# A router's threshold search in 16 turned rows per expert, two bits per level, with places from running sums

## The chip, the core and the metric

The kernel runs on one core of a Trainium2 chip. The metric is the device time of one execution in microseconds (us). The engines are PE (TensorE, matmul), DVE (VectorE), ACT (ScalarE), POOL (GpSimd) and SP (SyncE, which only issues DMAs).

## What is computed

Two layers, each a cross-attention and a feed-forward part with residuals, on `x` of 8 x 512 x 256. The last part is the one that the change touches: a mixture of 8 experts over all N = 4096 tokens, each expert taking at most 512 of them.

```python
probs = softmax(xf @ gate_w.T)                      # [4096, 8]
# per token: experts by falling probability, until their sum reaches 0.9
select_prefix = arange(E)[None, :] <= k_idx[:, None]
R_sorted = where(select_prefix, p_sorted - rank, -1e9)
# per expert: the 512 tokens of highest R (ties: the earlier token)
topC = argsort(-R, axis=0)[:C, :]
scores_sel = where(assign_mask & keep, probs, 0)
h = gelu(einsum('nd,efd->enf', xf, w1)); y_e = einsum('enf,edf->end', h, w2)
y = einsum('ne,end->nd', scores_sel, y_e)
```

## The kernel before

The program is a row of blocks: `setup` (constants), `mlstm_gates`, `mix_and_mlp`, `attention` (the longest), `logits`, `router`, `experts`. Between two blocks all engines meet. Inside a block each engine has its own written order, and semaphores order them against each other. On DVE the helper `v(ins)` lets every instruction wait for the one before.

Tokens lie as 128 partitions x NT = 32 tiles; `key` holds for each token and expert the value rank + 1 - p (low is good), and a huge value (FAR) where the token does not choose the expert. The router (L1237 to L1448) works thus:

- Softmax (L1351 to L1356), then pairwise comparisons of the 8 probabilities of a token into `pair_a` (L1363, L1365, and a memset of the diagonal, L1367); its sum is the rank, and its product with the probabilities, summed, is the probability mass `before` this expert (L1370 to L1372). L1374 to L1380 make `key`.
- PE turns `key` (L1317), so that an expert is 32 rows of 128 keys, four experts in each of two halves: `key_rows` [128, 2, 128].
- A search of 27 levels, one bit each, finds for each expert the largest threshold below which fewer than 512 keys lie. A level is on DVE two counts (L1393, a compare that also sums along its row), on PE one matmul with the 0/1 matrix `group` that adds the rows of an expert (L1323), on DVE the decision (L1399) and the next candidate (L1401). Beside levels 8 to 23 PE turns one half of an expert's weights each (`turn_weights`, L1312, four transposes), which ACT copies out (L1299).
- The thresholds are spread to all partitions (L1407 to L1411). Then, in the unturned layout, the keys below the threshold are counted (L1384, L1385), and `ranks` (L1418 to L1423: two matmuls, eight running sums) runs twice: once to pick the ties that still fit, once for each chosen token's place. L1438 to L1446 split the place into `chunk` (place / 128) and `slot`.

`experts` (L1451) copies `slot` to bf16 (L1648), builds on DVE one-hot matrices per expert (L1595 to L1610), gets the token list by matmul, gathers the token rows by indirect DMA on POOL (L1490), runs the two maps on PE, and adds the rows to the output by indirect DMA on POOL (L1501).

## Time and profile before

| what | value |
|---|---|
| median of 3 runs | 1900.68 us (1900.4 to 1904.55) |
| the profiled execution | 1900.8 us, of which its span is 1899.1 us |
| PE busy / DVE / ACT / POOL | 1708.0 / 1205.3 / 844.2 / 619.8 us |
| mean granted TensorE clock | 0.93 of full speed |

The busy shares are means over all blocks; the change lies in one of them. The rows of a timeline give the start of an instruction in us from the span's start, its length, engine, line, operation and tiles; in brackets stands how long the engine had been idle before it, and who ended that.

### The profile page before, as it was taken

The numbers are of one execution on the slowest core, as the hardware profiler recorded it, in microseconds if no ns is written. First come the engines' busy times: TensorE is split into PE (matmuls) and PEld (weight loads), VectorE is DVE, ScalarE is ACT, GpSimd is POOL, SyncE is SP. The second block draws the span as 40 slices with busy tenths as digits, with TensorE's granted clock in tenths as the row PEclk, the third lists the DMA queues.
The fourth block names the chain that finished last, engine by engine and source line by source line (L and its number), as shares of the span: only waits on it lengthen the run. The fifth ranks groups of instructions, "written<-read, shape, count | busy, mean of one in ns | idle before, by whom it ended". The sixth has DMA issues, their size and how long they took to land. (4 is left out here: it accounts for less than half of the span.)

```text
span 1899.1 us, 26206 instructions
## 1 busy us (share of the span) xinstructions
PE 1708.0 (90%) x8900; PEld 1157.0 (61%) x8900; DVE 1205.3 (63%) x2743; ACT 844.2 (44%) x1870; POOL 619.8 (33%) x745
## 2 busy tenths in 40 slices
PE   6569999996999999999999999999999999674484
PEld 4456677764666666666666666666666666472252
DVE  5443444431677777777777777777777777657761
ACT  3223443331555555555555555555555555211110
POOL 2143544440233333332323323333233233200385
PEclk9659999998999999999999999999999999855697
DMA  7100000003223222232231322323222223070154
GB/s 252 20 12 23 12 12 1 1 1 102 59 53 67 47 66 64 48 67 52 61 67 45 67 56 56 67 45 67 60 52 67 49 63 67 23 236 14 38 86 57
DMA packets 66658, 109.47 MB, mean 58 GB/s; under 512 B 16088, under 2 KB 48096, under 8 KB 66528
## 3 DMA queue, kind: packets, MB, share of 16 engines
...
q8 instruction: 72, 1.18, 0.3%
q14 instruction: 58, 0.48, 0.1%
...
## 5 line engine op out<-in xcount | busy, mean ns | idle before, releaser
L1018 POOL TENSOR_SCALAR at_Pr<-at_Pr,at_rinv 128x512 f32<-128x512 f32 x512 | 355.8, 695 | 824.4 <-DVE at_rinv L1045 824.4
L997 ACT ACTIVATE at_Pr<-at_ps,at_nmax 128x512 f32<-128x512 f32 x512 | 351.9, 687 | 522.6 <-DVE at_nmax L1040 521.0
L1040 DVE TENSOR_REDUCE at_nmax<-at_ps 128x1 f32<-128x512 f32 x512 | 351.1, 686 | 138.1 <-PE at_ps L905 127.3
L905 PE MATMUL at_ps<-at_k,at_q 128*128 128x512 f32 x1024 | 420.6, 492 | 9.6 <-DMA at_k<-at_k_own 7.9
L916 PE MATMUL at_ps<-k_ident,at_Pr 128*128 128x128 f32 x2048 | 310.7, 274 | 4.4 <-POOL at_Pr L1018 4.4
L916 PEld LDWEIGHTS at_ps<-k_ident,at_Pr 128*128 128x128 f32 x2048 | 249.3, 140 | 94.2 <-POOL at_Pr L1018 33.2
L1052 DVE COPY at_PT<-at_ps 128x512 f32<-128x512 f32 x384 | 261.5, 681 | 0.0
L905 PEld LDWEIGHTS at_ps<-at_k,at_q 128*128 128x128 f32 x1024 | 174.3, 190 | 128.9 <-issue 119.4
L926 PE MATMUL at_ps<-at_PT,at_V 128*64 128x512 f32 x1024 | 235.4, 602 | 0.9 <-DVE at_PT L1052 0.9
L1045 DVE RECIPROCAL at_rinv<-at_rsum 128x1 f32<-128x1 f32 x512 | 83.4, 163 | 175.0 <-ACT at_Pr L997 173.0
L926 PEld LDWEIGHTS at_ps<-at_PT,at_V 128*64 128x64 f32 x1024 | 68.2, 137 | 122.5 <-issue 121.4
L936 PE MATMUL at_ps<-at_wo,at_oT 128*128 128x256 f32 x512 | 131.6, 380 | 0.8 <-ACT at_oT L983 0.8
L446 PE MATMUL mm_ps<-mx_w,mm_hT 128*128 128x256 f32 x512 | 120.9, 382 | 0.0
L436 PE MATMUL mm_ps<-m_xnT,mx_w 128*128 128x512 f32 x256 | 112.8, 599 | 1.3 <-ACT m_xnT L589 1.3
L893 PE MATMUL at_ps<-at_w_rest,m_ctxT 128*128 128x128 f32 x896 | 109.2, 275 | 0.0
L884 PE MATMUL at_ps<-m_xnT,at_w_rest 128*128 128x512 f32 x224 | 106.3, 597 | 0.0
L884 PE MATMUL at_ps<-m_ctxT,at_w_rest 128*128 128x512 f32 x224 | 105.4, 593 | 0.0
L893 PEld LDWEIGHTS at_ps<-at_w_rest,m_ctxT 128*128 128x128 f32 x896 | 104.5, 192 | 0.0
L446 PEld LDWEIGHTS mm_ps<-mx_w,mm_hT 128*128 128x128 f32 x512 | 93.7, 190 | 16.6 <-issue 5.3
L1027 DVE SCALAR_TENSOR_TENSOR at_q<-at_ps,m_b_all,at_q 64x512 fp32r<-64x512 f32 x128 | 96.0, 750 | 8.6 <-ACT at_q L966 5.7
L997 ACT ACTIVATION_READ_ACCUMULATOR at_Pr<-at_ps,at_nmax 128x1 f32 x512 | 98.5, 192 | 0.0
L936 PEld LDWEIGHTS at_ps<-at_wo,at_oT 128*128 128x128 f32 x512 | 87.4, 190 | 8.3 <-ACT at_oT L983 1.7
...
## 6 DMA issues: line engine op xcount, KB each, us to landing
at_k<-at_k_own SPq DMA_DIRECT2D x256, 256.0 KB, 4.3
...
```

Source lines behind the costliest of these rows:

```text
L436: ins = pe.matmul(ps[:, H_BANK + f % 4, :], w1_s[:, k, P * f:P * f + P], xnT_all[:, k, b * S:b * S + S], start=k == 0, stop=k == DC - 1)
L446: ins = pe.matmul(ps[:, Y_BANK + t // 2, D * (t % 2):D * (t % 2) + D], hT[:, f, P * t:P * t + P], w2_s[:, f, :], start=f == 0, stop=f == F ...
L884: ins = pe.matmul(ps[:, A_BANK + k, :], weights(k, d, hp), src[:, d, b * S:b * S + S], start=d == 0, stop=d == DC - 1)
L893: ins = pe.matmul(ps[:, A_BANK, P * t:P * t + P], ctxT_all[:, d, b * S + P * t:b * S + P * t + P], weights(2, d, hp), start=d == 0, stop=d ...
L905: ins = pe.matmul(ps[:, S_BANK + j % 2, :], q2[:, u % 2, h, q:q + P], k2[:, u % 2, h, part, :], start=part == 0, stop=part == 1)
L916: ins = pe.transpose(ps[:, T_BANK + j % 2, P * t:P * t + P], Pr[:, j % 4, P * t:P * t + P], c["ident"][:, :])
L926: ins = pe.matmul(ps[AD * h:AD * h + AD, O_BANK, :], V[:, u % 2, t, AD * h:AD * h + AD], PT[:, u % 2, h, t, :], start=t == 0, stop=t == TP ...
L936: ins = pe.matmul(ps[:, Y_BANK - half, D * (t % 2):D * (t % 2) + D], oT[:, P * t:P * t + P], wo_s[:, u % HP, :], start=True, stop=True)
L997: act.activation(Pr[:, j % 4, :], ps[:, S_BANK + j % 2, :], ACT.Exp, bias=nmax[:, j % 4:j % 4 + 1], accum_out=rsum[:, j % 4:j % 4 + 1]).th ...
L1018: pool.tensor_scalar(Pr[:, n % 4, :], Pr[:, n % 4, :], rinv[:, n % 4:n % 4 + 1], 1.0, ALU.mult, ALU.mult).then_inc(s["pn"], 1)
L1040: dve.tensor_reduce(nmax[:, j % 4:j % 4 + 1], ps[:, S_BANK + j % 2, :], AX.X, ALU.max, negate=True).then_inc(s["nmax"], 1)
L1052: dve.tensor_copy(PT[:, u % 2, j // TPB, :, q:q + P], ps[:, T_BANK + j % 2, :].rearrange("p (t q) -> p t q", t=TPB)).then_inc(s["pt_v"], 1)
```

## The change

It touches `setup`, `router` and the first lines of `experts`; the kernel's other lines and all DMAs stay.

- `setup`: the constants `lower`, `ones_bf` and `earlier` go; `group` (now 0/1 blocks of 16 rows) and a new `group_ahead` (the rows in front, within a block) are made on POOL by three dependent selects and cast on DVE.
- The diagonal of the pair matrix (now `ahead`) is cleared by one memset while ACT computes the exponentials. Of the product with the probabilities POOL takes 14 of the 32 tiles and DVE 18; `key` takes three instructions besides these sums, one of them ahead of `before`, where it took six behind it.
- `key` is turned by parity of the tile: all 8 experts lie in 128 rows, 16 rows of 256 keys each.
- The search first decides one bit (4.0), then 13 levels of two bits: three candidates at once, three counts over 256 keys, one matmul of three columns, a compare that sums the three answers into a digit, and one addition to `T`. From its seventh matmul on PE turns both halves of an expert's weights per level.
- The thresholds need no spreading. In the turned rows two counts (below, equal) give masks, two running sums over 256 give places within a row, two small matmuls give each row's offset, and two pairs of matmuls with the identity turn the places back and add the two parts. Three instructions make `chunk` and a bf16 `slot_b`, and the first instruction of `experts` on DVE adds 1 to the comparison line.

```diff
 def setup(nc, c):
...
-                dve.memset(c["group"][:, :], 0.0).then_inc(s["cleared"], 1)
-                dve.wait_ge(s["cleared"], 1)
...
+                dve.wait_ge(s["made"], GROUP)
+                dve.tensor_copy(c["group"][:, :], same[:, :])
+                dve.wait_ge(s["made"], AHEAD_OF)
+                dve.tensor_copy(c["group_ahead"][:, :], ahead[:, :])
...
+                blocks = same[:, :].rearrange("p (g r) -> p g r", r=NT // 2)
+                pool.affine_select(out=blocks, in_=blocks, compare_op=ALU.is_ge, fill=0.0, base=0,
+                                   pattern=[[-NT // 2, E], [0, NT // 2]], channel_multiplier=1
+                                   ).then_inc(s["made"], 1)
+                pool.wait_ge(s["made"], HALF)
+                pool.affine_select(out=blocks, in_=blocks, compare_op=ALU.is_ge, fill=0.0, base=NT // 2 - 1,
+                                   pattern=[[NT // 2, E], [0, NT // 2]], channel_multiplier=-1
+                                   ).then_inc(s["made"], 1)
+                pool.wait_ge(s["made"], GROUP)
+                pool.affine_select(out=ahead[:, :], in_=same[:, :], compare_op=ALU.is_gt, fill=0.0,
+                                   base=0, pattern=[[1, P]], channel_multiplier=-1).then_inc(s["made"], 1)
...
-        STEPS = list(range(2, -25, -1))
+        FIRST = 2
+        LEVELS = list(range(FIRST - 2, -25, -2))
...
+            @block.gpsimd
+            def _(pool):
+                pool.wait_ge(s["ahead"], 1)
+                pool.tensor_tensor(weighed[:, 0:BY_POOL, :, :], ahead[:, 0:BY_POOL, :, :],
+                                   prob[:, 0:BY_POOL, :].rearrange("p t (a e) -> p t a e", a=1).broadcast_to(
+                                       [P, BY_POOL, E, E]), ALU.mult).then_inc(s["weighed"], 1)
...
                 pe.wait_ge(s["key"], 1)
-                for half in range(2):
-                    ins = pe.transpose(ps[:, 2, P * half:P * half + P],
-                                       key_e[:, HALF * half:HALF * half + HALF, :].rearrange("p e t -> p (e t)"),
-                                       c["ident"][:, :])
+                by_parity = key_e[:, :, :].rearrange("p e t -> p (e t)").rearrange("p (m r) -> p r m", r=2)
+                for r in range(2):
+                    ins = pe.transpose(ps[:, KEY_BANK, P * r:P * r + P], by_parity[:, r, :], c["ident"][:, :])
                 ins.then_inc(s["key_ps"], 1)
-                for n in range(len(STEPS)):
+                for n in range(len(LEVELS) + 1):
                     pe.wait_ge(s["count"], n + 1)
-                    pe.matmul(ps[:, 0, 0:2], c["group"][:, :], cnt2[:, :], start=True, stop=True
+                    width = 3 if n else 1
+                    pe.matmul(ps[:, FOUND_BANK, 0:width], c["group"][:, :], cnt[:, 0:width], start=True, stop=True
                               ).then_inc(s["found"], 1)
                     if n == WEIGHTS_AT:
                         pe.wait_ge(ew["loaded"], 16 * 2 * E)
-                    if WEIGHTS_AT <= n < WEIGHTS_AT + 2 * E:
-                        turn_weights(n - WEIGHTS_AT)
...
+                    if WEIGHTS_AT <= n < WEIGHTS_AT + E:
+                        turn_weights(2 * (n - WEIGHTS_AT))
+                        turn_weights(2 * (n - WEIGHTS_AT) + 1)
+                pe.wait_ge(s["count"], len(LEVELS) + 2)
+                pe.matmul(ps[:, OFFS_BANK, 0:2], c["group_ahead"][:, :], cnt[:, 0:2], start=True, stop=False,
+                          skip_group_check=True)
+                pe.matmul(ps[:, OFFS_BANK, 1:2], c["group"][:, :], cnt[:, 0:1], start=False, stop=True,
+                          skip_group_check=True).then_inc(s["offs_ps"], 1)
+                pe.wait_ge(s["placed"], 1)
+                for r in range(2):
+                    pe.matmul(ps[:, PLACE_BANK, P * r:P * r + P], place[:, 0, P * r:P * r + P], c["ident"][:, :],
+                              start=r == 0, stop=False, skip_group_check=True)
+                pe.wait_ge(s["placed"], 2)
+                for r in range(2):
+                    ins = pe.matmul(ps[:, PLACE_BANK, P * r:P * r + P], place[:, 1, P * r:P * r + P], c["ident"][:, :],
+                                    start=False, stop=True, skip_group_check=True)
+                ins.then_inc(s["placed_ps"], 1)
...
+                dve.memset(ahead[:, :, :, :].rearrange("p t a b -> p t (a b)")[:, :, 0:E * E:E + 1], 0.0)
+                dve.memset(T[:, :], 0.0)
+                dve.memset(cand[:, :], 2.0 ** FIRST)
                 dve.wait_ge(s["exp"], 1)
                 v(dve.tensor_reduce(red[:, 1, :], lg[:, :, :], AX.X, ALU.add))
                 v(dve.reciprocal(red[:, 2, :], red[:, 1, :]))
                 dve.tensor_tensor(prob[:, :, :], lg[:, :, :], over_e(red[:, 2, :]), ALU.mult).then_inc(s["prob"], 1)
                 dve.wait_ge(s["prob"], 1)
-                pj = prob[:, :, :].rearrange("p t (a e) -> p t a e", a=1).broadcast_to([P, NT, E, E])
                 for e in range(E):
                     own = prob[:, :, e:e + 1]
                     if e:
-                        dve.tensor_tensor(pair_a[:, :, e, 0:e], prob[:, :, 0:e], own.broadcast_to([P, NT, e]), ALU.is_ge)
+                        ins = dve.tensor_tensor(ahead[:, :, e, 0:e], prob[:, :, 0:e], own.broadcast_to([P, NT, e]),
+                                                ALU.is_ge)
                     if e < E - 1:
-                        ins = dve.tensor_tensor(pair_a[:, :, e, e + 1:E], prob[:, :, e + 1:E],
+                        ins = dve.tensor_tensor(ahead[:, :, e, e + 1:E], prob[:, :, e + 1:E],
                                                 own.broadcast_to([P, NT, E - 1 - e]), ALU.is_gt)
-                    dve.memset(pair_a[:, :, e, e:e + 1], 0.0)
-                v(dve.memset(T2[:, :], 0.0))
...
+                ins.then_inc(s["ahead"], 1)
+                dve.wait_ge(s["ahead"], 1)
+                dve.tensor_reduce(rank[:, :, :], ahead[:, :, :, :], AX.X, ALU.add)
+                v(dve.tensor_tensor(weighed[:, BY_POOL:NT, :, :], ahead[:, BY_POOL:NT, :, :],
+                                    prob[:, BY_POOL:NT, :].rearrange("p t (a e) -> p t a e", a=1).broadcast_to(
+                                        [P, NT - BY_POOL, E, E]), ALU.mult))
+                v(dve.scalar_tensor_tensor(out=key, in0=rank[:, :, :], scalar=1.0, in1=prob[:, :, :],
+                                           op0=ALU.add, op1=ALU.subtract))
+                dve.wait_ge(s["weighed"], 1)
+                v(dve.tensor_reduce(before[:, :, :], weighed[:, :, :, :], AX.X, ALU.add))
+                v(dve.tensor_scalar(flat(far), flat(before), 0.9, FAR, ALU.is_ge, ALU.mult))
+                dve.tensor_tensor(key, key, far[:, :, :], ALU.add).then_inc(s["key"], 1)
                 dve.wait_ge(s["key_ps"], 1)
-                v(dve.tensor_copy(key_rows[:, :, :], ps[:, 2, 0:2 * P].rearrange("p (a q) -> p a q", a=2)))
-                for k, bit in enumerate(STEPS):
-                    for half in range(2):
-                        ins = dve.tensor_scalar(below[:, half, :], key_rows[:, half, :], cand[:, half:half + 1], 0.0,
-                                                ALU.is_lt, ALU.add, accum_out=cnt2[:, half:half + 1])
+                v(dve.tensor_copy(key_rows[:, :], ps[:, KEY_BANK, 0:2 * P]))
+                def count(bound, op, at, mask):
+                    return dve.tensor_scalar(mask, key_rows[:, :], bound, 0.0, op, ALU.add,
+                                             accum_out=cnt[:, at:at + 1])
+                count(cand[:, 0:1], ALU.is_lt, 0, below[:, 0, :]).then_inc(s["count"], 1)
+                dve.wait_ge(s["found"], 1)
+                v(dve.tensor_scalar(T[:, :], ps[:, FOUND_BANK, 0:1], float(CAP), 2.0 ** FIRST, ALU.is_lt, ALU.mult))
+                for k, bit in enumerate(LEVELS):
+                    v(dve.scalar_tensor_tensor(out=cand[:, :], in0=c["slot"][:, 1:4], scalar=2.0 ** bit,
+                                               in1=T[:, :].broadcast_to([P, 3]), op0=ALU.mult, op1=ALU.add))
+                    for j in range(3):
+                        ins = count(cand[:, j:j + 1], ALU.is_lt, j, below[:, j, :])
                     ins.then_inc(s["count"], 1)
-                    if k:
-                        v(dve.tensor_tensor(T2[:, :], T2[:, :], step[:, :], ALU.add))
...
+                    dve.wait_ge(s["found"], k + 2)
+                    v(dve.tensor_scalar(hit[:, :], ps[:, FOUND_BANK, 0:3], float(CAP), 0.0, ALU.is_lt, ALU.add,
+                                        accum_out=digit[:, :]))
+                    v(dve.scalar_tensor_tensor(out=T[:, :], in0=digit[:, :], scalar=2.0 ** bit, in1=T[:, :],
+                                               op0=ALU.mult, op1=ALU.add))
+                count(T[:, 0:1], ALU.is_lt, 0, below[:, 0, :])
+                count(T[:, 0:1], ALU.is_equal, 1, tie[:, :]).then_inc(s["count"], 1)
+                dve.wait_ge(s["count"], len(LEVELS) + 2)
+                ones = c["ones_row"][:, 0:2 * P]
+                dve.tensor_tensor_scan(run[:, 0, :], ones, below[:, 0, :], 0.0, ALU.mult, ALU.add)
+                v(dve.tensor_tensor_scan(run[:, 1, :], ones, tie[:, :], 0.0, ALU.mult, ALU.add))
+                dve.wait_ge(s["offs_ps"], 1)
+                v(dve.tensor_copy(offs[:, :], ps[:, OFFS_BANK, 0:2]))
+                for k, mask in enumerate((below[:, 0, :], tie[:, :])):
+                    dve.scalar_tensor_tensor(out=place[:, k, :], in0=run[:, k, :], scalar=offs[:, k:k + 1],
+                                             in1=mask, op0=ALU.add, op1=ALU.mult).then_inc(s["placed"], 1)
+                dve.wait_ge(s["placed_ps"], 1)
+                at = ps[:, PLACE_BANK, 0:2 * P].rearrange("p (r e u) -> p r e u", r=2, e=E)
+                v(dve.tensor_scalar(part[:, :, :].rearrange("p (u r) e -> p r e u", r=2), at, 1.0 / P,
+                                    -(P - 1) / 2.0 / P - 1.0 / P, ALU.mult, ALU.add))
+                v(dve.tensor_scalar(flat(chunk), flat(part), ROUND, ROUND, ALU.add, ALU.subtract))
+                v(dve.scalar_tensor_tensor(out=slot_b[:, :, :].rearrange("p (u r) e -> p r e u", r=2),
+                                           in0=chunk[:, :, :].rearrange("p (u r) e -> p r e u", r=2),
+                                           scalar=-float(P), in1=at, op0=ALU.mult, op1=ALU.add))
...
-                dve.tensor_copy(ps[:, LINE_BANK, 0:P], c["slot"][:, :])
-                dve.tensor_copy(slot_b[:, :, :], slot[:, :, :]).then_inc(s["narrow"], 1)
+                dve.tensor_scalar(ps[:, LINE_BANK, 0:P], c["slot"][:, :], 1.0, None, ALU.add).then_inc(s["narrow"], 1)
```

How the instructions stand now. First DVE, the start of the search: before, from `key_rows` over the first two levels.

```order
L1390 COPY ro_key_rows<-ro_ps 128x256
L1393 TENSOR_SCALAR ro_below,ro_cnt<-ro_key_rows,ro_cand 128x128 x2
L1399 TENSOR_SCALAR ro_step<-ro_ps 128x2
L1401 SCALAR_TENSOR_TENSOR ro_cand<-ro_step,ro_T 128x2
L1393 TENSOR_SCALAR ro_below,ro_cnt<-ro_key_rows,ro_cand 128x128 x2
L1397 TENSOR_TENSOR ro_T<-ro_T,ro_step 128x2
```

A bit costs two counts of 128 keys there, with the addition to T behind them. The same place now, over the single bit and the first level of two:

```order
L1403 COPY ro_key_rows<-ro_ps 128x256
L1406 TENSOR_SCALAR ro_below,ro_cnt<-ro_key_rows,ro_cand 128x256
L1411 TENSOR_SCALAR ro_T<-ro_ps 128x1
L1413 SCALAR_TENSOR_TENSOR ro_cand<-k_slot,ro_T 128x3
L1406 TENSOR_SCALAR ro_below,ro_cnt<-ro_key_rows,ro_cand 128x256 x3
L1419 TENSOR_SCALAR ro_hit,ro_digit<-ro_ps 128x3
L1421 SCALAR_TENSOR_TENSOR ro_T<-ro_digit,ro_T 128x1
```

A level has three long counts for two short ones, and the addition to T, which stood behind the counts, now stands between the decision and the next candidate.

Second PE, in the search (`ro_cnt` the counts, `r_w` the experts' weights). Now:

```order
L1336 MATMUL ro_ps<-ro_cnt,k_group 128x1
L1336 MATMUL ro_ps<-ro_cnt,k_group 128x3 x6
L1325 MATMUL ro_ps<-k_ident,r_w 128x128 x8
L1336 MATMUL ro_ps<-ro_cnt,k_group 128x3
L1325 MATMUL ro_ps<-k_ident,r_w 128x128 x8
```

There are eight transposes of weights behind a counting matmul where there were four; the last eight stand behind the last of the 14 matmuls.

Third DVE, from the last threshold to the block's end. Now (the first row belongs to the last level):

```order
L1421 SCALAR_TENSOR_TENSOR ro_T<-ro_digit,ro_T 128x1
L1406 TENSOR_SCALAR ro_below,ro_cnt<-ro_key_rows,ro_T 128x256
L1406 TENSOR_SCALAR ro_tie,ro_cnt<-ro_key_rows,ro_T 128x256
L1428 SCALAR_TENSOR_TENSOR ro_run<-k_ones_row,ro_below 128x256
L1429 SCALAR_TENSOR_TENSOR ro_run<-k_ones_row,ro_tie 128x256
L1431 COPY ro_offs<-ro_ps 128x2
L1433 SCALAR_TENSOR_TENSOR ro_place<-ro_run,ro_offs,ro_below 128x256
L1433 SCALAR_TENSOR_TENSOR ro_place<-ro_run,ro_offs,ro_tie 128x256
L1437 TENSOR_SCALAR ro_part<-ro_ps 128x16x16
L1439 TENSOR_SCALAR k_token_chunk<-ro_part 128x256
L1440 SCALAR_TENSOR_TENSOR k_token_slot<-k_token_chunk,ro_ps 128x16x16
```

Before, 31 rows stood here, from L1403 to L1448, 46 instructions with the 16 short running sums; now ten stand behind the last L1421 (L1428 and L1429 are running sums).

## Rows read from the trace of the kernel before

**Rows 1.** Timeline of POOL: the first gather of expert 0, and of expert 2.

```profile
1775.61 1.25 POOL L1490 DMA_INDIRECT ex_xg<-rows,ex_idx_get  x1 [99.03 <-DVE ex_idx_get L1625]
...
1794.96 0.95 POOL L1490 DMA_INDIRECT ex_xg<-rows,ex_idx_get  x1 [7.43 <-DVE ex_idx_get L1625]
```

**Rows 2.** Timeline of DVE: first comparison, rank, sum of key (the last before turning).

```profile
1699.57 0.39 DVE L1365 TENSOR_TENSOR ro_pair_a<-k_prob 128x224 f32<-128x224 f32 x1
...
1702.83 2.29 DVE L1370 TENSOR_REDUCE ro_rank<-ro_pair_a 128x256 f32<-128x2048 f32 x1
...
1712.04 0.59 DVE L1380 TENSOR_TENSOR ro_key<-ro_key,ro_t 128x256 f32<-128x256 f32 x1
```

**Rows 3.** Groups by form, DVE: count | busy us, mean ns of one | idle before.

```profile
L1393 DVE TENSOR_SCALAR_CACHE_REDUCE ro_below<-ro_key_rows,ro_cand 128x128 f32<-128x128 f32 x54 | 16.6, 345 | 1.0
...
L1644 DVE TENSOR_SCALAR ex_y<-ex_ps,ex_sc 128x256 f32<-128x256 f32 x32 | 13.7, 479 | 18.7 <-PE ex_ps L1553 17.6 <-issue 0.7
...
L1371 DVE TENSOR_TENSOR ro_pair_a<-ro_pair_a,k_prob 128x2048 f32<-128x2048 f32 x1 | 2.3, 2291 | 0.0
...
L1420 DVE TENSOR_TENSOR_SCAN ro_offs<-k_ones_row,ro_tot 128x32 f32<-128x32 f32 x16 | 2.1, 201 | 0.1
...
L334 DVE TENSOR_TENSOR_SCAN mg_cums<-k_ones_row,mg_fg 32x512 f32<-32x512 f32 x1 | 1.2, 1212 | 0.0
...
L1377 DVE TENSOR_TENSOR ro_key<-ro_rank,k_prob 128x256 f32<-128x256 f32 x1 | 0.6, 596 | 0.0
...
L1374 DVE TENSOR_SCALAR ro_sel<-ro_before 128x256 f32<-128x256 f32 x1 | 0.3, 295 | 0.0
```

**Rows 4.** Timeline of the mixing block: POOL and DVE together, then DVE alone.

```profile
189.41 2.76 POOL L644 TENSOR_TENSOR mm_hs<-mm_hs,mx_w_row 128x256 f32<-128x256 f32 x4
189.48 2.84 DVE L73 TENSOR_SCALAR mm_xn<-k_x,mm_mv,mm_rstd 128x256 f32<-128x256 f32 x4 [1.19 <-POOL mm_rstd L85]
...
192.31 2.18 POOL L649 TENSOR_TENSOR k_x<-k_x,mm_hs 128x1024 f32<-128x1024 f32 x1
...
203.07 1.38 DVE L73 TENSOR_SCALAR mm_xn<-k_x,mm_mv,mm_rstd 128x256 f32<-128x256 f32 x4
```

**Rows 5.** Timeline of DVE: the search's first count, one level, the search's end.

```profile
1713.94 0.35 DVE L1393 TENSOR_SCALAR_CACHE_REDUCE ro_below<-ro_key_rows,ro_cand 128x128 f32<-128x128 f32 x1
...
1716.21 0.16 DVE L1399 TENSOR_SCALAR ro_step<-ro_ps 128x2 f32<-128x2 f32 x1 [0.28 <-PE ro_ps L1323]
...
1716.61 0.35 DVE L1393 TENSOR_SCALAR_CACHE_REDUCE ro_below<-ro_key_rows,ro_cand 128x128 f32<-128x128 f32 x1
...
1716.88 0.34 DVE L1393 TENSOR_SCALAR_CACHE_REDUCE ro_below<-ro_key_rows,ro_cand 128x128 f32<-128x128 f32 x1
...
1717.58 0.16 DVE L1399 TENSOR_SCALAR ro_step<-ro_ps 128x2 f32<-128x2 f32 x1 [0.28 <-PE ro_ps L1323]
...
1750.77 0.37 DVE L1407 TENSOR_SCALAR ro_T_diag<-k_ident,ro_T 128x4 f32<-128x4 f32 x2
```

**Rows 6.** Timeline of PE: eight transposes in `logits`; four in the search.

```profile
1654.23 1.94 PE L1180 MATMUL lo_ps<-k_ident,lo_xn 128*128 128x128 f32 x8 [5.63 <-DVE lo_xn L73]
...
1725.49 0.18 PE L1323 MATMUL ro_ps<-ro_cnt,k_group 128*128 128x2 bf16 x1 [1.18 <-DVE ro_below L1393]
1725.53 1.09 PE L1312 MATMUL ro_ps<-k_ident,r_w 128*128 128x128 f32 x4
```

**Rows 7.** Timeline of DVE: after the key's turning; the start of `experts`.

```profile
1713.48 0.42 DVE L1390 COPY ro_key_rows<-ro_ps 128x256 f32<-128x256 f32 x1 [0.85 <-PE ro_ps L1317]
...
1767.27 0.29 DVE L1647 COPY ex_ps<-k_slot 128x128 f32<-128x128 f32 x1 [0.55 <-PEq L1282]
...
1767.79 0.29 DVE L1595 TENSOR_TENSOR ex_is_chunk<-k_slot,k_token_chunk 128x128 f32<-128x128 f32 x1
```

**Rows 8.** Timeline of POOL in `setup`: the first select, after a wait for memsets.

```profile
2.15 0.29 POOL L123 TENSOR_SCALAR_AFFINE_SELECT k_ident<-k_ident 128x128 f32<-128x128 f32 x1 [0.25 <-POOL k_earlier L121]
```

**Rows 9.** Stretch of `experts`: length, PE, PEld, DVE, ACT, POOL busy, PEclk, DMA share, GB/s.

```profile
1797.00:1880.00 83.00, 63.81 (x385) 42.07 (x383) 44.92 (x92) 15.88 (x28) 65.13 (x51) 0.98 0.53 80
```

163 lines of the change are left out of this document (41 added, 122 removed).

## Prediction

> **What bounds the kernel now.** I asked first what the end of the program waits for. The chain that ended last is POOL's indirect DMAs, so I looked at what starts them. The first gather found POOL idle for 99.03 us, until DVE's list of token numbers; the third expert's gather waits for DVE again, and from there POOL has work to the end [rows 1]. What DVE does between the end of `logits` and 1775.61 is thus on the path, and the whole change lies there. So the view to read is DVE's timeline, piece by piece: the pairs and the key [rows 2], the search [rows 5], the tail [rows 7]. The reader is to see that DVE waits in the search only for PE's small matmul (0.28 us a level), and that the work is a long row of short instructions whose fixed cost counts as much as their length. That PE is busy 90% of the whole span says nothing here.
>
> Two prices from the groups by form [rows 3]: a count over 128 keys takes 0.345 us and an instruction of like build over 256 elements 0.479, so 1.05 ns per element; 2,048 elements in 2.291 then leave 0.14 fixed. In the nine instructions from L1370 to the end of L1380, 9.80 us [rows 2], three take 2.29, three 0.596 and three 0.295 [rows 3], 9.55 in all; the rest is 0.03 in each of eight gaps between dependent instructions.
>
> **The change part by part.** All sums are against the profiled execution, 1900.8 us (span 1899.1), which lies 0.1 above the median of the runs.
>
> *Setup.* Three selects on POOL now wait for each other; the row has 0.25 idle in front of a select that waits for POOL itself [rows 8]. Two more such waits give 0 to 0.6; the rest balances. All DMAs start behind this block. I take +0.25.
>
> *Pairs.* Ten memsets leave the 3.26 us from 1699.57 to 1702.83 [rows 2]. The comparisons' 1,792 elements at 1.05 ns are 1.9; the other 1.4 belongs to 24 instructions, so ten equal shares would be 0.6. A memset waits for nothing, so less: I take 0.35, between 0.1 and 0.6. Three memsets return while DVE waits for ACT's exponential: 0, at most 0.3 (one L1374).
>
> *Key.* Before 9.80. Now rank 2.29, DVE's 1,152 elements of the product 0.14 + 1.21 = 1.35, the key 0.60, the sum 2.29, 0.295, 0.60, gaps 0.2: 7.6. Saved: 2.2. This holds if POOL's 896 elements are done in time. POOL added 1,024 elements in 2.18 [rows 4], so 1.9, and with a start at most 0.25 late [rows 8] it is done 2.15 behind DVE's comparisons; DVE's own product begins 2.29 behind them. What if they meet? Beside a POOL instruction four L73 took 2.84, alone 1.38 [rows 4]: whoever comes second waits. At worst POOL works at the slower pace of those rows (2.76 for 1,024) and is done at 2.6: +0.3. I take 0. The Trainium skill says it as a rule ("SBUF — State Buffer", Who interferes with whom): a DVE instruction with two SBUF inputs and a GpSimd instruction that reads SBUF exclude each other for the whole instruction. By that rule the two products can't overlap at all, and the sum would be 1882.5 in place of 1882.2 if POOL is the later one; the trace agrees with it on L73.
>
> *Turning of the keys.* Two transposes as before, from a source of step 2. I take 0; if PE read at half pace, up to +0.7 of the 0.85 that DVE waits there [rows 7].
>
> *Search.* Before: from 1713.94 to 1750.77, 36.83 us, a level 1.37 (1716.21 to 1717.58) [rows 5]. A count comes 0.27 behind the other (1716.61, 1716.88); of 256 keys it is 0.13 longer, 0.40. A level now has a third count (+0.40), two longer ones (+0.27), the addition to T on the path (+0.20, half of the 0.40 from 1716.21 to 1716.61, which held two such small instructions), and a decision that sums three answers (I take +0.05; 0 if the sum is free, 0.15 if it costs a read-out and a gap). That is 2.29. The first bit has one count and no old T: 1.37 - 0.27 - 0.20 + 0.13 = 1.03. In all 1.03 + 13 x 2.29 = 30.8. Saved: 6.0, for the digit's bounds 4.7 to 6.7.
>
> PE's eight transposes per level are new beside this. In `logits` eight took 1.94, in the search four took 1.09 [rows 6]; a level leaves 2.29 less the small matmul's 0.18 (same rows). They fit, with 0.17 spare. The last eight stand behind the last matmul, so the offsets' matmuls come about 2 us after it; DVE has two counts and two running sums to do until then, so they are hidden too. No DMA moves, and SP and ACT keep their orders: ACT copies two halves per level where it copied one.
>
> *Tail.* Before: from 1750.77 to the first build at 1767.79, 17.02 us [rows 5, 7]. Now: two counts with read-out and wait 0.94; two running sums over 256: 1.212 for 512 and 0.201 for 32 [rows 3] are 2.11 ns per element, so 0.67 each, 1.35 together; offsets 0.20; two instructions with a pointer over 256, 0.479 and a little overlap, 0.88; PE's turning back as the key's 0.85 [rows 7], and since the first pair runs beside the second instruction I take 0.9, at most 1.3; then 0.596 (a write that hops, as L1377), 0.295, 0.596 and gaps, 1.6. Together 5.9. The change of block takes 0.55 and the line 0.3 [rows 7]. 6.7 in all. Saved: 10.3.
>
> Sum: -0.25 + 0.35 + 2.2 + 6.0 + 10.3 = 18.6. Forecast: 1900.8 - 18.6 = **1882.2 us**. Everything in `experts` comes earlier by that, unchanged.
>
> **The rivals.** About 0.2% of the time, 3.8 us, is what a measurement of this kernel can tell from no change.
>
> 1. *The counts run at two elements per cycle.* L1374 does: 0.295 for 256 elements, where 0.14 + 0.27 would be 0.41 [rows 3]. Then 42 counts are 0.07 shorter: 2.8 us, **1879.4**. Against it: the count's 0.345 lies on a line with 0.479, as at one per cycle. Chance 0.04. The Trainium skill ("VectorE: DVE Perf Modes", the perf-mode tier table) gives `tensor_scalar` two per cycle for fp32 in SBUF, which would be this rival; its page "SBUF — State Buffer" leaves out the form that writes its accumulator, and the row goes with that.
>
> 2. *PE becomes the bound of the search.* At a quarter of 1.09 each, eight transposes are 2.2, and with the matmul and its loading 2.4 to 2.6 where a level has 2.29: +0.1 to 0.3 on eight levels, **1883.0 to 1884.6**. Against it: 1.94 for eight in a row. Chance 0.06.
>
> 3. *The gain does not reach the end*: a gather waits for something else that comes no earlier, above all a DMA. Then no change, **1900.8**. For it: the gathered rows come from memory that other DMAs write. Against it: POOL's wait is put down to DVE's list, with 99 us of it [rows 1], and the DMAs are issued long before. Chance 0.03.
>
> 4. *Slower: TensorE's clock in `experts`.* From 1797 to 1880 PE is busy 63.81 of 83 us at a granted clock of 0.98 [rows 9], the upper level, 2.4 GHz. If other work in front of it left the clock at the lower level, 1.2 GHz (0.5), through this stretch, these 63.8 would be some 125, 42 more than the stretch: **1924**. It decides once the mean clock there falls under 0.75. Against it: the matmuls that come directly before the stretch are the same, in the same order. Chance 0.03.
>
> **How the numbers follow.** My forecast has 0.84. Its own bounds: digit -0.7 to +1.3, setup -0.25 to +0.35, pairs +-0.25, turned keys up to +0.7, places up to +0.4, POOL up to +0.3; added up, 1881.0 to 1885.5. Rivals 1 and 2 (another 0.10) and half a us of gaps lengthen that to 1878.5 to 1886.5, which I give. Faster by over 0.2% are the forecast and rivals 1 and 2, 0.94; within it rival 3, 0.03; slower rival 4, 0.03.
>
> **What would show it.** Right: the first gather some 18.6 earlier, at about 1757; a count of 0.48, a level of 2.29, 31 us for the search; under 7 us from the last threshold to the first build; DVE's product starting without a wait for POOL; PE's counting matmul still waiting for DVE in the levels with eight transposes. Wrong: a count of 0.41 (rival 1); a level longer from its seventh matmul on, with DVE waiting more than 0.28 for PE (rival 2); a gather that waits for a DMA (rival 3); a granted clock of 0.5 in `experts` (rival 4).

## The result and the profile after

| | before | after |
|---|---|---|
| four runs each on the same chip, median | 1900.54 us (1896.71 to 1904.55) | 1877.42 us (1875.32 to 1881.27) |
| ratio, 95% interval | | 0.9872 (0.985 to 0.9894) |
| profiled execution, time / span | 1900.8 / 1899.1 | 1875.32 / 1873.6 |
| router's first DVE instruction | 1696.83 | 1692.43 |
| from there to the first build | 70.96 | 51.25 |
| first build to the end | 131.30 | 129.94 |

The change makes the kernel faster by 23 us in this measurement; 1877.42 lies 4.8 below the forecast of 1882.2 and 1.1 below the range. The span is 25.5 shorter, and the last three lines of the table divide it: 4.40 come before the router, 19.71 in it, 1.36 behind it. I go through the router first. DVE's and POOL's timeline of the changed kernel, from the end of `logits` to the first count (start, duration, engine, line, instruction, and in brackets the idle time before it and what ended it):

```profile
1692.43 0.42 DVE L1368 TENSOR_REDUCE ro_red<-r_lg 128x32 f32<-128x256 f32 x1 [15.76 <-PEq L1136]
...
1695.10 0.39 DVE L1385 TENSOR_TENSOR ro_ahead<-k_prob 128x224 f32<-128x224 f32 x1
...
1698.10 2.29 DVE L1389 TENSOR_REDUCE ro_rank<-ro_ahead 128x256 f32<-128x2048 f32 x1
1698.14 2.08 POOL L1311 TENSOR_TENSOR ro_weighed<-ro_ahead,k_prob 128x896 f32<-128x896 f32 x1 [25.94 <-DVE ro_ahead L1382]
...
1700.30 1.35 DVE L1390 TENSOR_TENSOR ro_weighed<-ro_ahead,k_prob 128x1152 f32<-128x1152 f32 x1
...
1704.96 0.59 DVE L1399 TENSOR_TENSOR ro_key<-ro_key,ro_far 128x256 f32<-128x256 f32 x1
...
1706.80 0.48 DVE L1406 TENSOR_SCALAR_CACHE_REDUCE ro_below<-ro_key_rows,ro_cand 128x256 f32<-128x256 f32 x1
```

The pairs take 3.00 (1695.10 to 1698.10) where [rows 2] had 3.26, the key 7.45 where it had 9.80. POOL's product starts 0.04 behind DVE's reduction and ends at 1700.22, just before DVE's own product begins.

One level of the search, DVE with PE's small matmul:

```profile
1709.53 0.16 DVE L1419 TENSOR_SCALAR_CACHE_REDUCE ro_hit<-ro_ps 128x3 f32<-128x3 f32 x1 [0.28 <-PE ro_ps L1336]
...
1709.73 0.16 DVE L1421 SCALAR_TENSOR_TENSOR ro_T<-ro_digit,ro_T 128x1 f32<-128x1 f32 x1
1709.93 0.16 DVE L1413 SCALAR_TENSOR_TENSOR ro_cand<-k_slot,ro_T 128x3 f32<-128x3 f32 x1
1710.13 0.48 DVE L1406 TENSOR_SCALAR_CACHE_REDUCE ro_below<-ro_key_rows,ro_cand 128x256 f32<-128x256 f32 x1
...
1711.33 0.08 DVE L1406 DVE_READ_ACCUMULATOR ro_below<-ro_key_rows,ro_cand 128x1 bf16 x1
...
1711.48 0.18 PE L1336 MATMUL ro_ps<-ro_cnt,k_group 128*128 128x3 bf16 x1 [1.98 <-DVE ro_below L1406]
1711.70 0.16 DVE L1419 TENSOR_SCALAR_CACHE_REDUCE ro_hit<-ro_ps 128x3 f32<-128x3 f32 x1 [0.28 <-PE ro_ps L1336]
```

A level is 2.17 (1709.53 to 1711.70), averaged 2.165, and DVE waits 0.28 for PE as it did in [rows 5]. The search takes 29.11 us in place of 36.83.

The tail, DVE with PE's turning back, from the first count with the last threshold:

```profile
1735.91 0.48 DVE L1406 TENSOR_SCALAR_CACHE_REDUCE ro_below<-ro_key_rows,ro_T 128x256 f32<-128x256 f32 x1
...
1738.74 0.48 DVE L1433 SCALAR_TENSOR_TENSOR ro_place<-ro_run,ro_offs,ro_tie 128x256 f32<-128x256 f32 x1
...
1738.88 0.86 PE L1350 MATMUL ro_ps<-k_ident,ro_place 128*128 128x128 f32 x4 [1.82 <-DVE ro_place L1433]
...
1740.63 0.58 DVE L1437 TENSOR_SCALAR ro_part<-ro_ps 128x256 f32<-128x256 f32 x1 [1.41 <-PE ro_ps L1354]
...
1741.58 1.22 DVE L1440 SCALAR_TENSOR_TENSOR k_token_slot<-k_token_chunk,ro_ps 128x256 bf16<-128x256 f32 x1
...
1743.68 0.29 DVE L1588 TENSOR_TENSOR ex_is_chunk<-k_slot,k_token_chunk 128x128 f32<-128x128 f32 x1
```

From there (1735.91) to the first build it is 7.77 where [rows 5, 7] gave 17.02. PE's second pair of products follows the first from 1739.53, for 1.06. The wait for PE and the last instruction are the two rows that are longer than they were priced: 1.41 and 1.22.

PE in the levels with eight transposes of the weights, and the first gathers in `experts` on POOL with PE's first use of the rows:

```profile
1722.31 0.19 PE L1336 MATMUL ro_ps<-ro_cnt,k_group 128*128 128x3 bf16 x1 [0.18 <-DVE ro_below L1406]
1722.36 1.95 PE L1325 MATMUL ro_ps<-k_ident,r_w 128*128 128x128 f32 x8
...
1726.69 1.07 PE L1325 MATMUL ro_ps<-k_ident,r_w 128*128 128x128 f32 x8
...
1751.51 1.24 POOL L1483 DMA_INDIRECT ex_xg<-rows,ex_idx_get  x1 [51.30 <-DVE ex_idx_get L1618]
...
1758.68 1.97 PE L1528 MATMUL ex_ps<-k_ident,ex_xg 128*128 128x128 f32 x8 [1.35 <-DMA ex_xg<-rows,ex_idx_get]
```

The counting matmul still waits for DVE, by 0.18 where the prediction had 0.17 as spare, later by more. The first gather is still released by DVE's list, 24.1 earlier than in [rows 1]. Four of the later gathers are put down to a DMA (in the profile of before, one), but with 0.30 of idle, which also stands between two gathers that wait for nothing; so no gather loses time to a DMA. PE's first transposes of the gathered rows wait 1.35, in the profile of before 2.58:

```profile
1784.03 1.97 PE L1535 MATMUL ex_ps<-k_ident,ex_xg 128*128 128x128 f32 x8 [2.58 <-DMA ex_xg<-rows,ex_idx_get]
```

So three questions were open: where the 4.4 us ahead of the router come from, which step of the router's sum had the wrong size, and whether the 1.36 behind it belong to the change.

### The profile page after: what moved, and what is told of

The parts are those of the page before. It is cut to its first block and busy times, and to the rows that moved or that the text cites. A ratio compares the mean times of both kernels' runs of the same rounds, so it can differ in the third digit from the quotient of the medians.

```text
span 1873.6 us, 26058 instructions
## 1 busy us (share of the span) xinstructions
PE 1695.3 (90%) x8890; PEld 1150.4 (61%) x8890; DVE 1191.2 (64%) x2640; ACT 842.8 (45%) x1870; POOL 620.0 (33%) x746
```

## Experiments

### Both kernels again: is the time ahead of the router the change's?

No edit. Two theories: one execution against another, or the change's new addresses and constants.

> The changed kernel once more. Its profile began the router 4.4 us earlier than the profile of before (1692.43 against 1696.83), in code that the change does not touch. Theory A, one execution against another: the granted clock of TensorE in the first 150 us differs from execution to execution, so this repeat may begin the router anywhere from 1692 to 1701, with the stretch at the upper clock near 80 us longer where it begins earlier; the ratio to before tends to what the changed code alone gives, -19.7 in the router, -1.4 behind it, +0.4 in the setup: 0.989 (1880). Theory B, the change's other tile addresses or constants make the first stage faster: the router begins at 1692.4 +-0.5 again and the ratio is 0.9867 (1875.5). In both the router takes 51.2 to 51.3 us.

> The kernel before once more, as a profile. Theory A: the router begins anywhere from 1692 to 1701, and the single times lie on steps some 4 us apart, as 1896.71, 1900.4 and 1904.55 did. Theory B: it begins at 1696.8 +-0.5 each time. In both the router takes 70.9 to 71.1 us and the time from the first build of the one-hot to the end 131.3; if that last one comes out nearer to 129.9, the 1.4 us behind the router are scatter as well.

> The kernel before a third time, for one point: in its two profiles PE waited 2.58 and 2.77 us for the first expert's gathered rows, in six of the seven profiles with the new router 1.0 to 1.4, and in one 3.06. In the slow ones a packet of 16 KB of the instruction queue, which starts some 6.3 us behind the first gather in all of them, came in front of the gather's last packet. Theory A (which of them comes first is chance): this profile may show 1.2 to 1.4 us or 2.6 to 3.1. Theory B (the kernel before always meets it): 2.6 to 2.8 again, and the 1.3 us are a gain of the change.

> The changed kernel a third time, for its ratio to before. From the traces: -19.2 to -19.7 in the router, by the clock at which the places are turned back, +0.4 in the setup, 0 to -1.3 at the first gather: -18.8 to -20.6, a ratio of 0.989 to 0.990. The router begins anywhere from 1689 to 1701 in this profile. If the first measurement (0.9872) was right and the second (0.9893) was not, it is 0.987 again.

Measured: the changed kernel's median was 1880.48 (1878.03 to 1881.4), ratio 0.9893 (0.9874 to 0.9912), and the third time 1880.21 (1875.2 to 1880.68), ratio 0.9887 (0.9869 to 0.9905). The kernel before against itself gave 0.9998 (0.9985 to 1.001), its single times running from 1895.58 to 1904.03. Its third time, of a single execution, was 1891.51.

The windows of the trace from 60 to 125 us, the mean granted clock being the third figure from the right, for before, for after, for after again and for before a third time, the last two each with the router's first instruction on DVE's timeline; the same two rows follow for the run `slot` below, whose code up to the router is that of the changed kernel:

```profile
60.00:125.00 65.00, 38.05 (x190) 32.95 (x191) 29.15 (x51) 14.52 (x46) 23.55 (x23) 0.55 0.10 23
```
```profile
60.00:125.00 65.00, 36.16 (x204) 31.14 (x204) 31.22 (x54) 14.63 (x46) 23.54 (x23) 0.61 0.11 23
```
```profile
60.00:125.00 65.00, 37.85 (x185) 32.92 (x187) 29.07 (x50) 14.62 (x46) 23.05 (x23) 0.55 0.10 23
```
```profile
1697.97 0.42 DVE L1368 TENSOR_REDUCE ro_red<-r_lg 128x32 f32<-128x256 f32 x1 [15.76 <-PEq L1136]
```
```profile
60.00:125.00 65.00, 37.18 (x223) 32.58 (x224) 30.77 (x53) 14.27 (x46) 23.57 (x23) 0.68 0.11 23
```
```profile
1687.97 0.42 DVE L1351 TENSOR_REDUCE ro_red<-r_lg 128x32 f32<-128x256 f32 x1 [15.76 <-PEq L1126]
```
```profile
60.00:125.00 65.00, 35.66 (x202) 30.62 (x202) 31.69 (x55) 14.63 (x46) 23.54 (x23) 0.61 0.11 23
```
```profile
1696.70 0.42 DVE L1369 TENSOR_REDUCE ro_red<-r_lg 128x32 f32<-128x256 f32 x1 [15.76 <-PEq L1136]
```

Read the clock beside the start: 0.55 and 1696.83 (before), 0.61 and 1692.43 (after), 0.55 and 1697.97 (after), 0.68 and 1687.97 (before). The same program starts its router 8.9 us apart in two executions, and the new one 5.5 apart, these four in the order of the clock granted to TensorE between 60 and 125 us. Most of the difference is there when `attention` starts: its first matmul on PE is at 457.24, 453.39, 458.17 and 447.79. Theory B is refuted: a repeat of the changed kernel starts later than all three profiles of before. The single times go the same way: of the twelve of before, the four at 1895.6 to 1895.8 had a mean clock over the whole span of 0.932 to 0.935, the eight from 1899.5 on 0.930 to 0.932. But this window does not order every run: `slot` has the 0.61 of after and starts its router 4.3 later. From 125 to 150 us its clock is 0.72 against 0.80, its `attention` starts 2.1 later, and as much again is lost within `attention`, which nothing here explains. So the rows make the clock the likely cause of most of the spread; no run held it still, and it is not shown by an edit. The router itself was 51.25, 51.60 and 51.60 in the three profiles of after and 70.96, 70.97 and 70.99 in those of before. The 0.35 is PE's turning back, 1.41 in one and 1.77 in the others (below).

PE's wait for the first gathered rows was 2.58, 2.77 and 2.27 in the three profiles of before, 1.35, 1.39 and 1.40 in the three of after. Theory A had left room for 1.2 to 1.4 in the third; it did not come, so B has the better of it, and from first build to end it is 131.30, 131.01 and 130.84 against 129.94, 130.03 and 129.69: 1.2 us. Of the other runs below six waited 1.03 to 1.44, too, but one (`slot`) with the same code at this place waited 3.06, and from its first build to the end it is 130.92, as in the kernel before. The trace of the transfers has one packet of the instruction queue (0.02 MB) among the gather's last ones. Before, 1781.2 to 1783.6, and after, 1757.6 to 1759.0, each in 40 slices, in GB/s:

```profile
GB/s 0 0 484 141 211 211 141 211 211 493 211 71 0 0 0 0 0 0 0 0 0 0 0 70 0 0 0 0 0 0 70 0 0 0 0 0 0 0 0 0
```
```profile
GB/s 362 362 241 121 241 363 241 0 0 0 0 0 0 0 468 0 0 0 0 0 0 0 0 0 0 0 0 0 0 0 0 0 0 0 0 0 0 0 0 0
```

In after the instruction packet is the last to start (468 GB/s in a slice of 0.035 us are 16 KB), 0.25 behind the bulk of the gather. In before it starts in the third slice (the 484), ahead of the bulk's end, and two packets of the gather come 0.7 and 1.1 us behind that end. This suggests that they stood behind it, but the order alone is not the cause: in two of the other runs (`base` and `lean2` below) the packet also starts before the gather's last ones, 6.2 to 6.3 behind the gather, and PE waits 1.03 and 1.04. Why the wait is long in all three profiles of before and in one of ten with the new router stays open, so these 1.2 us are measured but not explained.

### One bit a level: what do the two bits bring by themselves?

```diff
-        LEVELS = list(range(FIRST - 2, -25, -2))
+        LEVELS = list(range(FIRST - 1, -25, -1))
...
-                    width = 3 if n else 1
+                    width = 1
...
+                    v(dve.tensor_scalar(cand[:, 0:1], T[:, :], 2.0 ** bit, None, ALU.add))
+                    count(cand[:, 0:1], ALU.is_lt, 0, below[:, 0, :]).then_inc(s["count"], 1)
+                    dve.wait_ge(s["found"], k + 2)
+                    v(dve.tensor_scalar(digit[:, :], ps[:, FOUND_BANK, 0:1], float(CAP), 2.0 ** bit, ALU.is_lt, ALU.mult))
+                    v(dve.tensor_tensor(T[:, :], T[:, :], digit[:, :], ALU.add))
```

> The changed kernel, but with the search by one bit a level: 27 levels of one count of 256 keys, the step taken by one instruction and added to T by the next. It tells what the two bits bring beside the turned layout alone. From the rows of the changed kernel a level is a count 0.40, read-out to decision 0.36, three small dependent instructions 0.60: 1.36. 27 of them are 36.7 us in place of 29.1. Theory 1, the gain of the search comes from fewer trips through PE and DVE's small instructions: +7.6 us, the search as long as in the kernel before (36.8). Rival, it comes from the turned layout (one count of 256 keys in place of two of 128): a level of 1.2 or less, the search at 32 or under.

Measured: the router takes 59.08, 7.5 more than the 51.60 of the changed kernel at the same turning back; a level is 1.35. DVE, one level:

```profile
1712.59 0.16 DVE L1416 TENSOR_SCALAR ro_digit<-ro_ps 128x1 f32<-128x1 f32 x1 [0.28 <-PE ro_ps L1336]
...
1713.17 0.48 DVE L1406 TENSOR_SCALAR_CACHE_REDUCE ro_below<-ro_key_rows,ro_cand 128x256 f32<-128x256 f32 x1
...
1713.94 0.16 DVE L1416 TENSOR_SCALAR ro_digit<-ro_ps 128x1 f32<-128x1 f32 x1 [0.28 <-PE ro_ps L1336]
```

Of this level only 0.40 is counting; 0.95 is the trip through PE and the small instructions, and that is paid 27 times. The search is 36.58, as long as in the kernel before (36.83): the turned layout alone brings it next to nothing, the two bits bring its gain. Theory 1 held.

### Sixteen transposes a level: how near is PE?

```diff
-                    if WEIGHTS_AT <= n < WEIGHTS_AT + E:
-                        turn_weights(2 * (n - WEIGHTS_AT))
-                        turn_weights(2 * (n - WEIGHTS_AT) + 1)
+                    if WEIGHTS_AT <= n < WEIGHTS_AT + E // 2:
+                        for k in range(4):
+                            turn_weights(4 * (n - WEIGHTS_AT) + k)
```

> The changed kernel with sixteen transposes of the weights in each of four levels in place of eight in each of eight. It tells how far PE is from the bound. At the lower clock eight take 1.95 and sixteen 3.9; a level has 2.16 and the small matmul stands behind them. Theory 1 (PE is hidden by 0.17 a level, and only just): the first levels with sixteen become 4.1 to 4.2 us, DVE waits about 2 us for PE in each until the clock rises, where sixteen take 2.14 and a level 2.3 to 2.4; in all +2 to +8 us. Rival (transposes overlap with the rest and PE has far more room): levels stay at 2.16, +0.

Measured: the router takes 53.85, 2.25 more; PE and DVE in the first two such levels:

```profile
1723.76 3.65 PE L1325 MATMUL ro_ps<-k_ident,r_w 128*128 128x128 f32 x16
...
1727.28 3.13 PE L1325 MATMUL ro_ps<-k_ident,r_w 128*128 128x128 f32 x16
```
```profile
1727.48 0.16 DVE L1419 TENSOR_SCALAR_CACHE_REDUCE ro_hit<-ro_ps 128x3 f32<-128x3 f32 x1 [1.66 <-PE ro_ps L1336]
...
1730.48 0.16 DVE L1419 TENSOR_SCALAR_CACHE_REDUCE ro_hit<-ro_ps 128x3 f32<-128x3 f32 x1 [1.11 <-PE ro_ps L1336]
```

DVE waits 1.66 and then 1.11 for PE in place of 0.28; the first such level is 3.55, less than the 4.1 expected, since sixteen in a row take 3.65 and not twice the 1.95 of eight; the granted clock over them is still 0.50. So the second rival of the prediction was a real bound that the change stays under. On the way the clock rises from 0.50 to 1.00, in the third and fourth such level sixteen take 1.95 and 1.94, and DVE's wait is 0.27 again. In the changed kernel eight go from 1.95 to 1.07 likewise: there the granted clock is 0.87 on average from 1722 to 1736, and 0.74 over the same stretch of the router in both repeats; in the search of the kernel before it is 0.50 throughout.

### A small instruction out of the chain

This run is called `base`.

```diff
...
+                    if not last:
+                        v(dve.scalar_tensor_tensor(out=then[:, :], in0=c["slot"][:, 0:4], scalar=2.0 ** (bit - 2),
+                                                   in1=cand[:, 0:1].broadcast_to([P, 4]), op0=ALU.mult, op1=ALU.add))
                     dve.wait_ge(s["found"], k + 2)
...
-                    v(dve.scalar_tensor_tensor(out=T[:, :], in0=digit[:, :], scalar=2.0 ** bit, in1=T[:, :],
-                                               op0=ALU.mult, op1=ALU.add))
+                        v(dve.scalar_tensor_tensor(out=cand[:, :], in0=digit[:, :].broadcast_to([P, 4]),
+                                                   scalar=2.0 ** bit, in1=then[:, :], op0=ALU.mult, op1=ALU.add))
```

> The changed kernel with one small instruction less between a level's answers and the next level's counts: while PE counts, DVE writes four numbers T + j x (next level's unit), and the digit is then added to all four at once; the first of them is the new T. A level of the changed kernel is 2.165: three counts at 0.40, read-out to decision 0.36, and decision, T and candidates 0.60 in a chain. Theory 1 (the chain of small dependent instructions is on the path, 0.20 each, and the wait for PE, 0.28, has room for one): a level of 1.97, the search 2.4 shorter, 26.7 us. Rival (the new instruction delays the decision by as much): 29.1, no change.

Measured: a level of 2.06, between the two theories. DVE:

```profile
1705.56 0.09 DVE L1407 DVE_READ_ACCUMULATOR ro_below<-ro_key_rows,ro_cand 128x1 bf16 x1
1705.56 0.16 DVE L1421 SCALAR_TENSOR_TENSOR ro_then<-k_slot,ro_cand 128x4 f32<-128x4 f32 x1
1706.01 0.16 DVE L1424 TENSOR_SCALAR_CACHE_REDUCE ro_hit<-ro_ps 128x3 f32<-128x3 f32 x1 [0.30 <-PE ro_ps L1337]
```

0.20 leaves the chain, but the decision begins 0.45 behind the last read-out, not 0.37 (1711.33 to 1711.70 above). The kernel before has the addition to T at just this place:

```profile
1717.14 0.08 DVE L1393 DVE_READ_ACCUMULATOR ro_below<-ro_key_rows,ro_cand 128x1 bf16 x1
1717.14 0.15 DVE L1397 TENSOR_TENSOR ro_T<-ro_T,ro_step 128x2 f32<-128x2 f32 x1
```

From read-out to the decision at 1717.58 [rows 5] that is 0.44 too. So the prediction's level carried 0.07 that the change takes away. The total, 1869.01, is one execution, whose router began at 1688.82; it says nothing of the edit. But its tail shows something that the edit does not touch, the turning back at the upper clock (a granted clock of 1.00, where 0.50 is the lower of the two levels). DVE's first instruction behind PE, and the window of PE's products (clock third from the right):

```profile
1735.18 0.59 DVE L1446 TENSOR_SCALAR ro_part<-ro_ps 128x256 f32<-128x256 f32 x1 [0.85 <-PE ro_ps L1355]
```
```profile
1733.98:1735.18 1.20, 1.16 (x8) 0.97 (x8) 0.35 (x2) 0.00 (x0) 0.00 (x0) 0.99 0.00 0
```

DVE waits 0.85 at a granted clock of 0.99. In the repeats of the changed kernel it waits 1.77 at 0.50. In the profile of after it waits 1.41: the first pair began at 1.00 (1738.88 to 1739.31), the second ran at 0.50 (1739.53 to 1740.60).

### The places turned back straight into the order of the tokens

This run is called `slot`.

```diff
+                turned = ps[:, PLACE_BANK, 0:2 * P].rearrange("p (u r e) -> p r e u", r=2, e=E)
...
-                    pe.matmul(ps[:, PLACE_BANK, P * r:P * r + P], place[:, 0, P * r:P * r + P], c["ident"][:, :],
+                    pe.matmul(turned[:, r, :, :], place[:, 0, P * r:P * r + P], c["ident"][:, :],
...
-                v(dve.scalar_tensor_tensor(out=slot_b[:, :, :].rearrange("p (u r) e -> p r e u", r=2),
-                                           in0=chunk[:, :, :].rearrange("p (u r) e -> p r e u", r=2),
-                                           scalar=-float(P), in1=at, op0=ALU.mult, op1=ALU.add))
+                v(dve.scalar_tensor_tensor(out=flat(slot_b), in0=flat(chunk), scalar=-float(P), in1=at,
+                                           op0=ALU.mult, op1=ALU.add))
```

> The changed kernel with the places turned back by PE straight into the order of the tokens, so that DVE's three last instructions read and write row after row. In the changed kernel they take 0.58, 0.29 and 1.22. Theory 1 (the last one is long because it writes 16-bit numbers with a hop and reads two operands with a hop): 0.42 to 0.48, 0.29 and 0.48 to 0.60, and 0.7 to 0.9 us less in the tail, if PE's writes with a hop take no longer. Rival (it is long because it reads PSUM, or writes 16 bits): it stays near 1.2 and the tail is 0.1 shorter.

Measured, DVE:

```profile
1745.25 0.42 DVE L1438 TENSOR_SCALAR ro_part<-ro_ps 128x256 f32<-128x256 f32 x1 [1.77 <-PE ro_ps L1355]
...
1746.03 0.42 DVE L1440 SCALAR_TENSOR_TENSOR k_token_slot<-k_token_chunk,ro_ps 128x256 bf16<-128x256 f32 x1
```

1.22 became 0.42 and 0.58 became 0.42; PE's wait is the 1.77 of the changed kernel's repeats, so PE's writes with a hop cost nothing that the trace shows. The router is 50.63, 0.97 shorter. The order of access is the cause, neither PSUM nor the 16 bits alone; which of the hops was not separated: the 16-bit write, or the read of `chunk` (the other input, from PSUM, was read row after row in both kernels). The total was 1879.99, since this is the execution in which PE waited 3.06 for the gather.

### More of the product on POOL

```diff
-        BY_POOL = 14
+        BY_POOL = 22
```

> The changed kernel with 22 of the 32 token tiles of the product on POOL in place of 14. POOL's 896 elements took 2.08, so 1,408 take 3.27 and end 3.3 after DVE's reduction of the ranks begins; DVE's own product begins 2.2 after that point. So the two products now have to overlap by 1.1 us. Theory 1 (they run side by side): DVE's product 0.68 in place of 1.35, the key ready 0.67 earlier. Rival (one excludes the other, as the four L73 beside a POOL instruction suggested, and as the Trainium skill has it): DVE's product waits for POOL's end, is then 0.68, and the key comes 0.4 later than in the changed kernel.

Measured, DVE and POOL:

```profile
1703.89 3.15 POOL L1311 TENSOR_TENSOR ro_weighed<-ro_ahead,k_prob 128x1408 f32<-128x1408 f32 x1 [25.94 <-DVE ro_ahead L1382]
1706.05 1.68 DVE L1390 TENSOR_TENSOR ro_weighed<-ro_ahead,k_prob 128x640 f32<-128x640 f32 x1
```

POOL ends at 1707.04. DVE's 640 elements are issued at 1706.05 and end at 1707.73, 0.69 behind POOL's end: they waited. The rival held, and the router is 51.95, 0.35 longer than 51.60. The Trainium skill ("SBUF — State Buffer", Who interferes with whom) says that such a DVE instruction, with two inputs from SBUF, and a GpSimd instruction that reads SBUF exclude each other for the whole instruction; the trace agrees, 0.99 of the 1.68 being the wait. The L73 that the prediction took as agreement has one tensor and two numbers per partition as inputs, so it is not a case of two SBUF tensors; the product here is. DVE's reductions, with one input, ran beside POOL at their 2.29. The 14 tiles of the change end 0.08 before DVE's product begins, so giving POOL more tiles gains nothing at this place.

### Both edits, and PE's turning back

The first kernel, `lean2`, has the edits of `base` and `slot` together, with no wait of DVE for the small instruction. The second, `lean3`, has besides:

```diff
+                v(ins)
+                dve.tensor_tensor(place[:, 0, :], place[:, 0, :], place[:, 1, :], ALU.add).then_inc(s["placed"], 1)
...
+                    ins = pe.transpose(turned[:, r, :, :], place[:, 0, P * r:P * r + P], c["ident"][:, :])
```

> The changed kernel with the two edits together, and the four numbers of the next level written without a wait of DVE for them (the wait behind the decision covers them). Alone the first edit brought a level from 2.165 to 2.06, not 1.97: the decision began 0.45 after the last read-out in place of 0.36. Theory 1 (it was DVE's own wait for the small instruction in front of the wait for PE that held it up): a level of 1.97 to 2.0, the search 2.0 to 2.4 shorter than in the changed kernel, the tail 1.2 shorter, as in the run with the places turned into order, 3.2 to 3.6 in all and a ratio to before of 0.9875. Rival (the instruction itself stands in front of the decision): a level of 2.06, 2.5 us in all, 0.988.

> As the kernel sent with it, but DVE adds the two places and PE turns the sum with two transposes in place of two pairs of matrix products against the identity, each of which the trace lists as four instructions. In the changed kernel the time from the start of the second place to the first instruction behind PE is 0.48 + 1.41 = 1.89 at the upper clock and 0.48 + 1.77 = 2.25 at the lower. Now: the second place 0.40 to 0.48, the addition 0.59, PE as for the keys 0.80: 1.8 to 1.9 at the lower clock. Theory 1 (PE's passes are the cost): 0.3 to 0.4 us less than the kernel sent with it. Rival (PE's start and hand-over are the cost, as the second pair already runs in the first's shadow): the same or up to 0.3 longer.

Measured: a level of 1.97 in both, the decision again 0.37 behind the last read-out, so it was DVE's own wait for the small instruction that had cost the 0.07 to 0.08; routers of 48.30 and 47.78 where the changed kernel has 51.60. Medians 1880.16 (ratio 0.9896, 0.988 to 0.9913) and 1876.09 (0.9868, 0.9846 to 0.989). From the start of the second place to the first instruction behind PE, in the first and in the second kernel, the latter with PE's two transposes:

```profile
1739.52 0.48 DVE L1445 SCALAR_TENSOR_TENSOR ro_place<-ro_run,ro_offs,ro_tie 128x256 f32<-128x256 f32 x1
1741.76 0.42 DVE L1449 TENSOR_SCALAR ro_part<-ro_ps 128x256 f32<-128x256 f32 x1 [1.77 <-PE ro_ps L1356]
```
```profile
1741.46 0.48 DVE L1440 SCALAR_TENSOR_TENSOR ro_place<-ro_run,ro_offs,ro_tie 128x256 f32<-128x256 f32 x1
1741.97 0.42 DVE L1443 TENSOR_TENSOR ro_place<-ro_place 128x256 f32<-128x256 f32 x1
...
1742.45 0.69 PE L1352 MATMUL ro_ps<-k_ident,ro_place 128*128 128x128 f32 x2 [2.67 <-DVE ro_place L1443]
...
1743.17 0.42 DVE L1446 TENSOR_SCALAR ro_part<-ro_ps 128x256 f32<-128x256 f32 x1 [0.78 <-PE ro_ps L1352]
```

2.24 became 1.71, both at a granted clock of 0.50. A matrix product against the identity in fp32 is two of the trace's instructions for each 128 x 128 block where a transpose is one, and at this clock an addition of 0.42 on DVE is cheaper than the second pair. At the upper clock, in `base`, the way with the two pairs was 1.34, so this gain hangs on the clock; no run shows the two transposes at the upper one. By the traces theory 1 held in both, the second by more than expected; the ratio of 0.9875 that it gave the first kernel was not met.

By the traces the first kernel saves 3.3 us and its median moved 0.1 to 0.3 against the repeats of the changed kernel; the second saves 3.8 and its median moved 4.1 to 4.4. Against the first measurement of the changed kernel (1877.42) the first is 2.7 slower and the second 1.3 faster. With single times that spread over 5 to 9 us, five runs do not resolve 3 us. The second has the shortest router of all and the lowest median of what was run more than once, but by their intervals its ratio can't be told from the changed kernel's 0.9872.

## Why the prediction was wrong, and where it was right

**Right.** The mechanism and its places: the gain goes through to the first gather and to the end, and none of the four rivals came. A count is 0.48, not 0.41 (rival 1). DVE's wait for PE stays at 0.28 (rival 2), with the spare of 0.17 that was worked out, and the run with sixteen transposes shows that the bound was there. No gather loses time to a DMA (rival 3). In `experts` the granted clock is 0.98 from 1772.9 to 1855.9, the stretch of [rows 9] 24.1 earlier, and 0.98 there too (rival 4). POOL's product ended in time without a wait.

**The step that failed** is in two places. In the sum, three terms had the wrong size: the search saved 7.72 in place of 6.0, the tail 8.9 to 9.25 in place of 10.3, and `experts`, put at nothing, 1.2 to 1.4; together 1.6 to 2.1 more than the 18.6 (below). In "How the numbers follow", the range was built from the bounds of the change's own terms, "and half a us of gaps", and the profiled execution was set beside the median with a distance of 0.1. Nothing in it stood for the code that the change does not touch, which starts the router anywhere between 1687.97 and 1697.97 in the profiles of these two kernels. A median of four runs with two at 1875 and two at 1879 and 1881 lies 3 us under the medians of the same kernel in its two repeats, 1880.48 and 1880.21, which the range holds. One of the four, 1875.32, was profiled, and its router started 4.4 earlier than in the profile of before; that the other at 1875 was short for the same reason is likely and not shown. The three times of before that were known, 1900.4 to 1904.55, already lay 4 us apart, and the range did not use it.

**The terms**, with what the two profiles give:

| term | predicted | measured |
|---|---|---|
| setup (first DMA issued 3.89, then 4.28) | +0.25 | +0.39 |
| pairs | -0.35 | -0.26 |
| key | -2.2 | -2.35 |
| turning of the keys, softmax | 0 | -0.13 |
| search | -6.0 | -7.72 |
| tail | -10.3 | -9.25 (-8.9 in the repeats) |
| `experts` | 0 | -1.2 to -1.4 |
| sum | -18.6 | -20.2 to -20.7 |

Added to 1900.8, the measured terms give 1880.1 to 1880.6, which is where the medians of the repeats lie. That the forecast is only about 2 us from there is in part luck, since the errors of the search and of the tail have opposite signs. Three sizes were off:

- *Search.* "That is 2.29" was 2.165, 0.12 on each of 13 levels. The sum of three answers was given 0.05 and cost nothing: decision to T is 0.20, as for any two small dependent instructions. And the 0.44 from read-out to decision was carried over whole, though the old addition to T had lengthened it by 0.07; moved away from there, it leaves 0.37. With a small instruction put back at that place (`base`) it is 0.45, without DVE's own wait for it (`lean2`) 0.37 again.
- *Tail.* 6.7 was 7.77 (8.1 in the repeats). The turning back was taken from the keys' transposes, 0.9 and at most 1.3, which DVE waited for 0.85 at a granted clock of 0.50. Products against the identity are twice as many PE instructions: at the same clock 1.77, and 1.41 where the clock fell between the pairs, both past the bound. Only at the upper clock (`base`) is it 0.85. The expectation for `lean3`, which called the 1.41 a time at the upper clock, misread it. The last instruction, priced as a write with a hop at 0.596 by L1377, took 1.22; the run without the hops took 0.42. The change of block and the line were as forecast.
- *"Everything in `experts` comes earlier by that, unchanged"* was off by 1.2 to 1.4 us at the landing of the first expert's gather, whose cause is open.

The first two pull in opposite directions and leave 0.3 to 0.7 of the 1.6 to 2.1 us by which the sum was short; the rest is the last, with 0.1 of the smaller terms.
